# One stream over four batches: the loop around the main stage taken away, output projections moved into it, and the gated layer's pieces placed by a table of times

## The reference, cut to what matters

```
x = L0_attn_x                      # (4, 2048, 256) float32: 4 batches of 2048 tokens
xn = layernorm(x)
# causal attention, 16 heads of 16
q, k, v = split(xn @ Wqkv.T);  attn = softmax(mask(q k^T * 16**-0.5));  o = attn v
attention = o @ Wout.T + bout
# gated layer; fp4() rounds blocks of 16 values to a grid of 4-bit floats times a scale
gate = fp4(xn) @ fp4(w_gate).T     # 704 columns
up   = fp4(xn) @ fp4(w_up).T
layer = fp4(silu(gate) * up) @ fp4(w_down).T
out = x + attention + layer
```

## Time and profile before

| what | us |
|---|---|
| median of 3 runs | 2636.86 (2636.82 to 2639.11) |
| span of the profiled execution, first to last instruction | 2634.3 |
| what lies around that span | the page gives no device time for this execution; the runs lie 2.5 to 4.8 above its span |
| PE busy | 2291.5, 87% |
| ACT busy | 1991.2, 76% |
| DVE busy | 1901.9, 72% |

### The profile page before, as it was taken

How to read it: one execution, slowest core, us unless ns; L and a number is a source line. 1 busy time by engine, 2 the same in 40 slices (tenths; PEclk the granted TensorE clock), 3 DMA queues, 4 the chain that set the end, 5 groups by cost and what they waited for, 6 DMA issues and landing times.

```text
span 2634.3 us, 89616 instructions
## 1 busy us (share of the span) xinstructions
PE 2291.5 (87%) x34104; PEld 1276.1 (48%) x34104; DVE 1901.9 (72%) x5676; ACT 1991.2 (76%) x3470; POOL 645.3 (24%) x524
## 2 busy tenths in 40 slices
PE   2896999999999957888888888888888888888888
PEld 1784444444444424444445444545454445444455
DVE  6675999999999965656656666665676565566565
ACT  1343999999999957888875888885888884887885
POOL 3212233333333321212211222211122211222211
PEclk9897999999999989999999999999999999999999
DMA  2576445555555522011012011021111021110101
GB/s 61 177 227 143 69 73 72 73 73 72 73 73 72 73 36 64 21 22 30 23 47 62 18 27 30 16 57 50 24 31 30 15 60 45 27 30 16 27 18 34
DMA packets 94822, 144.19 MB, mean 55 GB/s; under 512 B 25264, under 2 KB 74160, under 8 KB 93872
## 3 DMA queue, kind: packets, MB, share of 16 engines
q1 hardware_dynamic: 73456, 113.77, 23.1%
q10 hardware_dynamic: 16576, 15.73, 1.9%
q0 software_dynamic: 4352, 8.92, 1.4%
HBM read 104.20 MB, written 34.14 MB: 53 GB/s over the span
## 4 chain that ended last, share of the span: by engine, by line
PE 31%; ACT 12%; issue 11%; DVE 7%; ACTq 1%; DMA 0%; SPq 0%; POOL 0%; DVEq 0%; POOLq 0%
ACT probs L1129 10%; PE O L998 8%; PE F L1019 8%; PE F L1059 6%; PE S L977 5%; PE S L1070 2%; PE F L1049 1%; DVE h_norm L1282 1%; DVE o_turned L1344 1%; DVE o_turned L1345 1%; ACT ht_hi L1144 1%; DVE fp_step L1280 1%; DVE fp_step L1278 1%; PE F L1012 1%; PE S L983 0%
## 5 line engine op out<-in xcount | busy, mean ns | idle before, releaser
L1129 ACT ACTIVATE probs<-S 128x1024 f32<-128x1024 f32 (+3 forms) x1280 | 1056.0, 907 | 143.6 <-issue 52.8
L775 ACT ACTIVATE m_excess<-m_DIFF 128x512 f32<-128x512 f32 (+7 forms) x1536 | 646.9, 472 | 85.7 <-PE m_DIFF L735 39.9
L793 DVE CUSTOM_DVE_ANT_0 m_excess<-m_S,m_excess 128x512 f32<-128x512 f32 (+7 forms) x1536 | 700.6, 530 | 11.8 <-PE m_S L735 9.5
L998 PE MATMUL O<-probs,v_sb 64*32 64x512 f32 (+3 forms) x10240 | 611.3, 534 | 33.3 <-DVE o_turned L1345 29.3
L977 PE MATMUL S<-q_st,k_st 64*32 64x512 f16 (+3 forms) x10240 | 432.2, 353 | 180.6 <-ACT probs L1129 140.9
L733 PE MATMUL m_S<-m_k,m_q 128*128 128x512 f16 (+7 forms) x1536 | 482.9, 325 | 26.7 <-DVE m_row_max L793 17.3
L733 PE MATMUL m_DIFF<-m_k,m_q_diff 128*128 128x512 f16 (+7 forms) x1536 | 477.7, 319 | 26.5 <-DMA m_q_diff<-s_q 26.2
L977 PEld LDWEIGHTS S<-q_st,k_st 64*32 64x32 f16 x10240 | 136.1, 90 | 588.7 <-ACT probs L1129 480.4
L677 POOL TENSOR_TENSOR m_q_diff<-m_zero,m_q 48x4096 f16<-48x4096 f16 x32 | 224.4, 7012 | 428.9 <-DMA m_q<-s_q 418.2
L733 PEld LDWEIGHTS m_S<-m_k,m_q 128*128 128x128 f16 x1536 | 148.3, 97 | 275.8 <-DVE m_row_max L793 195.1
L1307 DVE TENSOR_SCALAR tanh<-tanh 128x352 int32<-128x352 int32 x128 | 49.4, 386 | 273.9 <-ACT decay L1139 273.9
(11 more groups left out here) (178 smaller groups left out, 3923.0 us busy)
## 6 DMA issues: line engine op xcount, KB each, us to landing
m_q<-s_q SPq DMA_DIRECT2D x96, 128.0 KB, 3.8
m_k<-s_k SPq DMA_DIRECT2D x96, 128.0 KB, 6.7
m_q_diff<-s_q SPq DMA_DIRECT2D x96, 128.0 KB, 8.0
k_st<-s_k SPq DMA_DIRECT2D x96, 128.0 KB, 4.3
q_st<-s_q SPq DMA_DIRECT2D x384, 32.0 KB
m_k<-s_k SPq DMA_DIRECT2D x96, 124.0 KB, 5.3
a_x<-in_L_attn_x_dram POOLq DMA_DIRECT2D x16, 512.0 KB, 4.8
s_q<-a_part SPq DMA_DIRECT2D x32, 256.0 KB, 2.5
```

The source lines that it names most:

```text
L775: act.activation(excess[u % MAX_EXCESS][:, 0:keys // 2], DIFF[u % MAX_BUFS][:, 0:keys // 2], ACT.Relu) \
L793: dve.tensor_tensor_reduce(larger, S[u % MAX_BUFS][:, 0:keys // 2], larger, 1.0, -3e38, ALU.add, ALU.max, column).then_inc(reduced[u % MAX ...
L998: ins = pe.matmul(O[e][s * SLOT:(s + 1) * SLOT, st.skip:QC], v_sb[st.hg % 2][rows, st.j, s * SLOT:(s + 1) * SLOT], probs[s // 2][st.n % PR ...
L1129: act.activation(probs[half][st.n % PROBS][:, :, 0:st.width], S[half][:, :, 0:st.width], ACT.Exp, scale=scale).then_inc(exped[half], 1)
```

## The change

The main stage becomes one stream. The hardware loop is gone: every engine's instructions are written out for all four batches, with steps and tiles numbered through (`TILES` = 16, `ALL` = 64 tiles), and the tile n of the gated layer goes on across a batch's end.

The places are no longer k = 0 to 9. Each tile has 20 marks. A step costs its width + 110, a mark is due at an even share of a batch's cost, and it falls into the early or the late half of the step that holds its time; a table says at which mark each piece stands on each engine. With these numbers the pattern repeats every 4 tiles, that is every 40 steps.

On PE the pieces of a step now come ahead of the values. On ACT and DVE, early pieces stand between the two exponentials of the step, or ahead of `normalise`, and late ones behind them. `gate` and `up` have marks of their own (gate at 7 and 11, up at 9 and 13), `down` is cut in two halves of 9 matmuls (marks 19 and 1), and `h_turn` takes the tile before, not the one before that.

Output projections are two for each tile, from 3 tiles before a batch's end on for 8 tiles: `F[0]` at mark 0 and `F[1]` at mark 5, added by DVE at marks 2 and 7. The last batch has three such tiles; its other 10 projections follow the last step, as before. x is loaded into a ring of three (`x_in`), and the loads and stores of x and y go from ACT's queue to SP's, two tiles to a store. The scale table `norm` is loaded once for all batches.

```
@@ place of the pieces
-X_TURN_AT, PAIR_AT, FIRST_PAIR_AT = 2, {4: 0, 7: 1}, {5: 0, 8: 1}
-H_TURN_AT, DOWN_AT = 0, 2
+def place_marks(steps, b):
+    ends, total = [], 0
+    for st in steps:
+        total += st.width + STEP_COST
+        ends.append(total)
+    at = 0
+    for n in range(TILES):
+        for k in range(MARKS):
+            due = (n * MARKS + k + 0.5) * total / (TILES * MARKS)
+            while ends[at] <= due:
+                at += 1
+            half = ends[at] - (steps[at].width + STEP_COST) / 2
+            (steps[at].early if due < half else steps[at].late).append((b * TILES + n, k))
+X_TURN_AT = 4
+GATE_AT, UP_AT = ((7,), (11,)), ((9,), (13,))
+H_TURN_AT = 16
+DOWN_AT = (19, 1)
+X_HIGH_AT, GATE_PARTS_AT, H_HIGH_AT = 4, (8, 12), 16
+X_LOW_AT, SILU_AT, GATED_AT, H_LOW_AT, ADD_DOWN_AT = 5, (9, 13), (10, 14), 17, 3
+X_SCALES_AT, X_ROUND_AT, H_SCALES_AT, H_ROUND_AT = 6, 11, 15, 1
+PROJ_FROM, PROJ_TILES = TILES - 3, 8
+PROJ_AT = ((0,), (5,))
+PROJ_ADD_AT = (2, 7)
+def projected_at(t, side):
+    g = t - PROJ_FROM
+    if g < 0 or g % TILES >= PROJ_TILES:
+        return None
+    return g // TILES * TILES + 2 * (g % TILES) + side
@@ PE
+            def x_turn(t):
+                pe.wait_ge(x_ready, t + 1 + PRIMED)
+                if t >= 2:
+                    pe.wait_ge(ht_lo_done, 2 * (t - 2) + 1 + PRIMED)
+                if projected_at(t, 0) is not None:
+                    pe.wait_ge(y_final, projected_at(t, 0) + 1 + PRIMED)
...
+            for st in steps:
...
+                scores(st, 0)
+                scores(st, 1)
+                for t, k in st.early + st.late:
+                    pieces(t, k)
+                if st.n:
+                    values(steps[st.n - 1])
@@ ACT
+            for st in steps:
+                exps(st, 0)
+                for t, k in st.early:
+                    pieces(t, k)
+                exps(st, 1)
+                for t, k in st.late:
+                    pieces(t, k)
@@ DVE
-            with dve.Fori(0, B) as b:
+            for st in steps:
+                for t, k in st.early:
+                    pieces(t, k)
+                if st.n and steps[st.n - 1].last:
+                    normalise(steps[st.n - 1].chunk)
+                for t, k in st.late:
+                    pieces(t, k)
```

More of the change, by code:

```diff
@@ L850, in main_phase @@
     steps = attention_steps()
-    nsteps = len(steps)
-    chunks = NHG * NQC
+    chunks = B * NHG * NQC
     last_step = [st.n for st in steps if st.last]
-    tiles = T // P
-    per_tile = nsteps // tiles
-    assert per_tile == 10
     fb = D // QBLK
     hb = I // QBLK
+    inside = sum(projected_at(t, side) is not None for t in range(ALL) for side in range(2))
     primed = []
@@ L977, in scores @@
                         ins = pe.matmul(S[half][at, e, 0:st.width], k_st[p][rows, half, st.j * P + at.start:st.j * P + at.stop],
-                                        q_st[st.c % 2][rows, half, st.skip:QC], start=True, stop=not st.diagonal)
+                                        q_st[st.chunk % 2][rows, half, st.skip:QC], start=True, stop=not st.diagonal)
                 if st.diagonal:
@@ new lines, in _ @@
+            pe.wait_ge(consts, CONSTS)
+            for st in steps:
+                if st.c == 0 and st.first:
+                    pe.wait_ge(group_ld[st.group % 2], 16 * group_dmas * (st.group // 2 + 1) + PRIMED)
+                if st.first:
+                    pe.wait_ge(q_ld[st.chunk % 2], 16 * q_dmas * (st.chunk // 2 + 1) + PRIMED)
+                scores(st, 0)
+                scores(st, 1)
+                for t, k in st.early + st.late:
+                    pieces(t, k)
+                if st.n:
+                    values(steps[st.n - 1])
@@ new lines, in _ @@
+            values(steps[-1])
+            for piece in range(1, len(DOWN_AT)):
+                down(ALL - 2, piece)
+            for part in range(2):
+                h_turn(ALL - 1, part)
+            for m in range(inside, ALL):
+                if m - inside < SPARE:
+                    pe.wait_ge(exped[m % SPARE // 2], len(steps) + PRIMED)
+                else:
+                    pe.wait_ge(y_final, m - SPARE + 1 + PRIMED)
+                project(m, spare(m))
+                if m == inside + FLUSH_DOWN:
+                    for piece in range(len(DOWN_AT)):
+                        down(ALL - 1, piece)
@@ new lines, in _ @@
+            dve.wait_ge(norm_ld, 16)
+            x_scales(0)
+            x_round_(0)
+            for st in steps:
+                for t, k in st.early:
[3 more added lines that the diff above has]
+                for t, k in st.late:
+                    pieces(t, k)
+            h_round_(ALL - 1)
+            normalise(chunks - 1)
+            add_down(ALL - 2)
+            for part in range(2):
+                h_low(ALL - 1, part)
```

666 lines of the change are left out of this document (321 added, 345 removed).

## The result

The changed kernel took **2720.52 us** (median of 3 runs, 2720.27 to 2721.0) against 2636.86; the ratio is 1.031, with an interval of 1.0299 to 1.0327. Its profiled span is 2719.3.

The account below looks back on a forecast made before the run. Neither PE nor ACT was full; ACT idled in three gaps and on late inputs, with PE having 0.09 us slack a step. Terms -84 - 6 + 47 - 26 + 12 + 5 - 7 = -59 gave 2578 us, range 2500 to 2640.

Parts of the forecast that it names:

- The gaps, -84: Between batches: three gaps of 27.9 us, in which ACT does almost nothing, go; -84 us.
- The clock, -6: PE behind each gap: a 5 us stretch at clock 0.50 goes, taken as 2 us a batch; -6 us.
- Projections, +47: 54 projections moved into PE's steps, 0.87 us each, all paid because PE has 0.09 us slack; +47 us.
- DVE beside the projections: `x_turn` and `F[1]` projections wait for additions standing behind `normalise` on DVE; +12 us, ends 0 and 25.
- The gated layer's own pieces: Gate, up, `down`, turns and DVE waits in the steps: idle ACT 3.8 us a tile against 4.2; -26, ends -50 and 0.
- ht_hi: `ht_hi` of two tiles a batch, 0.76 us each, moves from the gap to ACT's stream; +5 us.
- Spacing gate and up: Gate and up in separate steps beside a late ACT piece: ACT idle 0.5 us a tile for both pairs.
- The tail, -7: After the last step: 10 projections instead of 16, and stores two tiles at a time; -7 us, 0 to -9.
- The start, nothing: Before the stream: larger `norm` and an x tile load ahead of keys, +1, x earlier, -1 to -4; counted as nothing.
- Rival 2: DVE's order becomes the bound, silu late in every tile, some 1.5 us more each; +96, so 2674 us; 15%.
- Rival 1: Spacing works better than the step-by-step reading, `down` hidden too; -102, so 2476 us; 20%.
- The fetch rule: Loop branches: a taken branch outside the fetched window stalls, straight code mostly doesn't; 8.6 us, already part of the -84.

Follow-up runs that it names:

- no_proj_split: split_norm without the 54 projections that stand in the stream and their additions; 2531.15 us, 0.959 of the kernel before.
- no_proj: The changed kernel without the 54 projections inside the stream, their additions and the waits for them; 2585.6 us, 0.981 of the kernel before.
- split_norm: adds_round with the wait for `k_st` back on PE and `normalise` split, all but its transposes a step later; 2578.24 us, 0.9775 of the kernel before.
- down_whole: adds_round with `down` whole at mark 19, 18 matmuls instead of two halves of 9; 2621.58 us, 0.994 of the kernel before.
- adds_round: Changed kernel with additions of `down` and second projection one mark earlier, rounding of h at mark 19 of its own tile; 2621.36 us, 0.994 of the kernel before.

## Why the prediction was wrong, by its own steps

I compare streams, from the first exponential to the end of the last, in the profiled executions. Before it is 1619.4; without its three gaps of 27.9, 1535.7.

| stream | us | against |
|---|---|---|
| before, without gaps | 1535.7 | |
| no_proj_split | 1518.6 | -17.1 |
| no_proj | 1567.6 | +31.9 |
| split_norm | 1568.1 | 49.5 above no_proj_split |
| changed kernel | 1703.5 | 135.9 above no_proj |

- **The gaps, -84: right.** Nothing like them is left. **The clock, -6: wrong in sign.** The stretches behind the gaps went, as forecast, but this term was all that I had for the clock, and 24 others came with the new waits: 116.0 us at 0.50 where there had been 34.1.
- **Projections, +47: right.** 47.1 in time, 49.5 in the stream, once nothing on DVE delays them. PE's lack of slack held here.
- **DVE beside the projections, +12 with ends 0 and 25: the step that failed most.** It came to 135.9 - 49.5 = 86. I went through the marks and looked for who waits for a late *addition of down* and who shares `F[0]`. I did not ask it of the addition into `F[1]` at mark 7, which stands late in the very step in which `normalise` comes, in tiles 14 and 16 and their like: 13 waits, 37.5 us by the rows, where my list has none. The places I named cost 20.4 and 7.8. And no term counted what a PE wait of 2 to 4 us costs in clock afterwards, though the earlier trace rows had shown it behind a gap. The 86 us are thus a wait that was left out and a cost of waits that was put at nothing.
- **The gated layer's own pieces, -26 with ends -50 and 0: wrong in sign.** With the clock and `ht_hi` terms it was to be -27 and came to +31.9. Two parts. The DVE part, 0.7 us a tile or 45, was sized rightly: no_proj less no_proj_split is 49.0. PE's part was not: with DVE's waits gone ACT is idle 380.1 - 316.85 = 63.3 us a batch, 3.95 a tile, where I had 3.1 (54 us over 64 tiles). down_whole points at the most of it: I let the second half of `down` off 0.5 us for standing in a late step and the first 0.09, so 1.6 for both; the rows of adds_round say 2.08. Most of the slack behind a late step isn't there. The rest, some 0.4 us a tile, is not traced to a piece.
- **Spacing gate and up: right in sign.** Together they cost 74 and 54 us more. What I expected of the first of the two runs, from 0.5 us a tile against 0.7 to 1.4, was 10 to 40.
- **An unwritten zero: PE's order.** The change puts pieces ahead of values, and I never priced it. With split_norm's table it is worth 105.6 us, more than any term of the sum; what it is worth in the changed kernel itself was not run.
- **ht_hi, +5**, is inside the -17.1 and not told apart. **The tail, -7:** -6.1. **The start, nothing: wrong, +7,** which is the wait on SP's queue: with it moved back to PE the first exponential came at 988.6 to 990.6 (six runs), and at 993.6 to 995.8 in the changed kernel and the five runs that kept it. The diff moved a wait from PE to the queue that issues the loads, and I read only what was issued, not what it waits for.

The sum of the misses is the whole: 77 beside the projections (135.9 against 47 + 12), 59 in the own pieces (31.9 against -27), 7 at the start, 1 in the tail, 144 in all, and 2719.3 - 2575 is 144.

That split_norm ran at 2578.24 and the forecast was 2578 is an accident. The forecast held 57 us for DVE's waits (45 + 12), of which split_norm has hardly any, and it was 54 too low in PE's part; the two errors cancel.

**The rivals.** Rival 2 had the right side and the right law: DVE runs in order, and nothing passes a late `normalise`. The rule that I cited for it (the Trainium skill, TensorE: Matmul & The Clock Gate, section Architectural detail, on the strict order of ACT's and DVE's queues) holds in the rows above, where a 0.4 us addition whose input had been ready for 5 us waits. Its place was wrong: it put the price on silu in every tile, which cost 19.3 us; the price was on the additions, in three of four tiles and for the most part in two. Rival 1 needed more slack on PE than the forecast gave it, and the forecast named such slack as what would make it wrong. There was none to be found; what failed is the order on DVE, the clock behind its waits and the price of PE's pieces. The fetch rule (the Trainium skill, Runtime: NRT & Kernel Launch, section Instruction fetch mechanics) gave 8.6 us for three branches. With the loops written out the three gaps shrank by 9.8, which agrees, though the register instructions went as well and the runs do not tell the two apart.

Not tried: a cure for the clock alone, with the waits left in, and a place for projections in which PE has time to spare.

## What to carry to other kernels

When work is moved into the stream of an engine that runs in order, list for each short instruction that somebody waits for what stands ahead of it, up to the last thing that *it* waits for, and split or postpone any long block (here 3.3 us of `normalise`, of which 1.3 were urgent). On PE put what the next engine waits for in this step ahead of what is only due in a later one; that was worth more than every move of work between steps tried here. And price a stall of the matmul engine as the stall and the half clock after it: here 60 us less of waiting, most of it in waits of 2 to 4 us, brought some 39 us more than itself, while the shorter waits of no_proj, up to 1.8 us, brought no half clock in that run.

## What the runs showed of the hardware that I had not expected

Short waits of PE are enough to bring the granted clock to 0.50, in stretches of 3.4 or 6.8 us. Of the 24 stretches in the changed kernel's stream, 17 began during or within 1.6 us behind one of the 19 waits of 2.5 to 3.8 us for the addition of a projection, 4 at waits of 1.43 us for that of `down`, 2 behind waits of 1.77 us for silu, and 1 at a pause of 2.62 us for issue. Length alone does not decide it: no_proj has eight waits of 1.76 us for silu and none is followed by such a stretch. Four projection matmuls took 2.08 us at 1413.91, starting 0.48 apart, where in the same stream at full clock four take 1.13 and start 0.25 apart. In adds_round and split_norm, whose 53 and 15 waits for DVE in the stream are 0.5 to 1.65 us long, there is a single such stretch, behind a pause of 2.23 us for issue, and the windows of a batch in split_norm show 0.99 to 1.00.
